# Selective scan of a graph network: steps alternate between the channel halves, decay factors in SBUF

## The reference, cut to what matters

```
dt  = softplus(dbc[:, :16] @ dt_proj_w.T + dt_proj_b)    # n x 256
Bm  = dbc[:, 16:32]; Cm = dbc[:, 32:]                    # n x 16 each
A   = -exp(A_log)                                        # 256 x 16
dA  = exp(dt[:, :, None] * A)                            # decay factors
dBx = (dt * xc)[:, :, None] * Bm[:, None, :]
def step(h, t):                                          # h: 256 x 16
    dA_t, dBx_t, C_t = t
    h = dA_t * h + dBx_t
    return (h, h @ C_t)
_, y = lax.scan(step, zeros, (dA, dBx, Cm))
y = (y + xc * D_param) * silu(z)
return y @ out_proj_w.T
```

## Time and profile before

| | us |
|---|---|
| median of 3 runs (7062.06 to 7075.2) | 7067.35 |
| the profiled execution's own time | 7078.49 |
| its span, from the first to the last instruction | 7076.8 |
| phase `mamb`: first load issued to the last projection | 2459.2 to 2877 |
| its loop: first scan to the end of the last product with C | 2469.76 to 2851.96 |

### The profile page before, as it was taken

The page is one execution under the profiler, slowest core; times in us unless marked ns, Lnnn a source line. Parts: engine busy times, 40 slices in busy tenths (PEclk is TensorE's granted clock), DMA queues, the critical chain, the costliest instruction groups (busy, mean ns, idle before and its releaser), DMA issues. The chain is left out here.

```text
span 7076.8 us, 83913 instructions
## 1 busy us (share of the span) xinstructions
PE 4376.6 (62%) x18956; PEld 2316.1 (33%) x18957; DVE 3988.4 (56%) x6332; ACT 1872.1 (26%) x2833; POOL 2303.0 (33%) x2173
## 2 busy tenths in 40 slices
PE   4888477233998266589656677456676444450387
PEld 2454366111443123465222333223333122220123
DVE  7987277598997699455222333122333122227998
ACT  1476111012886322244101111001111000110254
POOL 0000000410000066200466665666665666660000
PEclk8999687666999588799777888777887666665798
DMA  0471565434665377315555666555666444443444
GB/s 30 151 237 56 193 250 200 150 120 123 180 180 148 114 278 269 125 52 213 168 169 169 192 203 191 157 170 179 192 204 188 138 132 138 134 136 121 138 134 120
DMA packets 466391, 1139.22 MB, mean 161 GB/s; under 512 B 63000, under 2 KB 254255, under 8 KB 454409
## 3 DMA queue, kind: packets, MB, share of 16 engines
q1 hardware_dynamic: 294485, 543.98, 23.8%
q0 software_dynamic: 134816, 447.33, 21.3%
q10 hardware_dynamic: 36996, 146.80, 5.7%
HBM read 882.81 MB, written 258.28 MB: 161 GB/s over the span
## 5 line engine op out<-in xcount | busy, mean ns | idle before, releaser
L2693 POOL DMA_INDIRECT rel1s_rows<-rel_table,rel1s_at x640 | 625.7, 978 | 371.1 <-issue 289.0
L2693 POOL DMA_INDIRECT rel2s_rows<-rel_table,rel2s_at x640 | 616.0, 963 | 379.5 <-issue 222.1
L2693 POOL DMA_INDIRECT rel0s_rows<-rel_table,rel0s_at x640 | 625.7, 978 | 344.0 <-issue 284.6
L2895 PE MATMUL rel2s_acc<-rel2s_rows,rel2s_hot 128*128 x732 | 404.8, 563 | 483.2 <-issue 302.2
L2156 POOL TENSOR_TENSOR mamb_st<-mam_u,mamb_bc 128x1600 f32<-128x1600 f32 x64 | 236.7, 3699 | 1073.4 <-DMA mamb_bc<-dbc 1073.4
L1676 PE MATMUL gatx_acc<-gatx_w,gatx_feat 128*65 128x400 f32 x1600 | 541.3, 501 | 24.9 <-DVE gatx_w L1568 24.9
L2895 PE MATMUL rel0s_acc<-rel0s_rows,rel0s_hot 128*128 x732 | 317.8, 454 | 261.5 <-issue 183.1
L2895 PE MATMUL rel1s_acc<-rel1s_rows,rel1s_hot 128*128 x732 | 317.3, 452 | 238.9 <-issue 167.6
L1568 DVE SCALAR_TENSOR_TENSOR gatx_w<-gatx_w,gatx_adj 128x1600 f32<-128x1600 f32 x200 | 363.2, 1817 | 0.5 <-ACT gatx_w L1624 0.5
L1676 PE MATMUL latx_acc<-latx_w,latx_feat 128*65 128x400 f32 x800 | 291.0, 507 | 101.5 <-DVE latx_w L1568 101.5
L1415 DVE CUSTOM_DVE_ANT_0 gatm_junk<-gatm_srow,gatm_gone 128x3125 bf16<-128x3125 f32 x100 | 335.7, 3411 | 27.7 <-DMA gatm_srow<-gat_scores 23.4
(11 more groups left out here) (615 smaller groups left out, 9544.9 us busy)
## 6 DMA issues: line engine op xcount, KB each, us to landing
mamb_bc<-dbc SPq DMA_DIRECT2D x128, 800.0 KB, 5.6
agg_strip<-strips SPq DMA_DIRECT2D x100, 800.0 KB, 5.9
gatx_adj<-adj SPq DMA_DIRECT2D x200, 400.0 KB, 3.0
adj<-adj_counts SPq DMA_DIRECT2D x25, 1600.0 KB, 7.1
latx_adj<-adj SPq DMA_DIRECT2D x100, 400.0 KB, 3.1
rel_table<-rel0p_prod POOLq DMA_DIRECT2D x25, 1536.0 KB, 6.2
rel_table<-rel0s_prod ACTq DMA_DIRECT2D x25, 1536.0 KB
rel_table<-rel1s_prod ACTq DMA_DIRECT2D x25, 1536.0 KB
```

Source lines behind the costliest of these rows:

```text
L2693: pool.indirect_dma_start(rows[k][:, u, :], None, table, bass.IndirectOffsetOnAxis(ap=at[:, n:n + 1], axis=0)).then_inc(s_in[u], 16)
L2895: one = nc.tensor.matmul(acc[a][:, :], hots[k], most_two[k], start=fresh and k == 0, stop=False)
```

## The change

The 64 steps are ordered by node half, then state, then channel half: two steps in a row share their rows of B and C, which are loaded once for both (64 loads instead of 128; SP waits for the second of the two steps that used a buffer). Since two channel halves are now under way at a time there are two accumulators, which fill PSUM (4 banks each). The decay factors move from PSUM to SBUF, into two buffers of 128 x 1600, so that ACT waits for the scan two steps back. The last node half of both channel halves is now multiplied by silu(z) on DVE (8 instructions instead of 4), POOL has two output products in place of three, and the projection writes to the first accumulator.

```diff
@@ -2114,13 +2114,14 @@
-            acc = ph.ps("acc", [P, 4 * BANK])
-            dA = ph.ps("dA", [P, 4 * BANK])
+            dA = [ph.sb(f"dA{k}", [P, HALF]) for k in range(2)]
+            acc = [ph.ps(f"acc{ct}", [P, 4 * BANK]) for ct in range(2)]
...
-            todo = [(ct, half, n) for ct in range(2) for half in range(2) for n in range(S)]
+            todo = [(half, n, ct) for half in range(2) for n in range(S) for ct in range(2)]
+            rows = [(half, n, m) for half in range(2) for n in range(S) for m in range(2)]
@@ -2129,14 +2130,12 @@
-                for q, (ct, half, n) in enumerate(todo):
-                    for m in range(2):
-                        r = 2 * q + m
-                        if r >= RB:
-                            sp.wait_ge(s_hc if m else s_x, (r - RB) // 2 + 1)
-                        at = R + m * S + n
-                        sp.dma_start(bc[r % RB][:, :],
-                                     row(dbc_dram[at:at + 1, when(half)].rearrange("o n -> (o n)"))).then_inc(s_bc[r % RB], 16)
+                for r, (half, n, m) in enumerate(rows):
+                    if r >= RB:
+                        sp.wait_ge(s_hc if m else s_x, (r - RB) // 2 * 2 + 2)
+                    at = R + m * S + n
+                    sp.dma_start(bc[r % RB][:, :],
+                                 row(dbc_dram[at:at + 1, when(half)].rearrange("o n -> (o n)"))).then_inc(s_bc[r % RB], 16)
...
@@ -2146,84 +2145,82 @@
-                for q, (ct, half, n) in enumerate(todo):
-                    r = 2 * q
-                    if ct and not half and n == 0:
+                for q, (half, n, ct) in enumerate(todo):
+                    r = q // 2 * 2
+                    if q == 1:
                         pool.wait_ge(s_later, 2)
                     pool.wait_ge(s_bc[r % RB], 16 * (r // RB + 1))
                     if q >= RS:
                         pool.wait_ge(s_y, q - RS + 1)
                     nc.gpsimd.tensor_tensor(st[q % RS][:, :], u[:, ct, when(half)], bc[r % RB][:, :], ALU.mult).then_inc(s_x, 1)
-                    if q > S and n == 2:
-                        i = q // S - 1
-                        pool.wait_ge(s_copied, i + 1)
-                        at = when(i % 2)
-                        nc.gpsimd.tensor_tensor(yT[:, i // 2, at], yT[:, i // 2, at], dt[:, i // 2, at], ALU.mult).then_inc(s_yT, 1)
+                    if half and n == 2:
+                        pool.wait_ge(s_copied, ct + 1)
+                        nc.gpsimd.tensor_tensor(yT[:, ct, when(0)], yT[:, ct, when(0)], dt[:, ct, when(0)], ALU.mult).then_inc(s_yT, 1)
...
-                for q, (ct, half, n) in enumerate(todo):
-                    if ct and not half and n == 0:
+                for q, (half, n, ct) in enumerate(todo):
+                    if q == 1:
                         act.wait_ge(s_later, 2)
-                    if q:
-                        act.wait_ge(s_h, q)
-                    nc.scalar.activation(dA[:, 0:HALF], dt[:, ct, when(half)], ACT.Exp, scale=A[:, ct, n:n + 1]).then_inc(s_dA, 1)
-                    if q and n == 0:
-                        i = q // S - 1
-                        act.wait_ge(s_y, q)
+                    if q > 1:
+                        act.wait_ge(s_h, q - 1)
+                    nc.scalar.activation(dA[q % 2][:, :], dt[:, ct, when(half)], ACT.Exp, scale=A[:, ct, n:n + 1]).then_inc(s_dA, 1)
+                    if half and n == 0:
+                        act.wait_ge(s_y, 2 * S - 1 + ct)
                         for a, b in spans:
-                            last = nc.scalar.copy(dt[:, i // 2, (i % 2) * HALF + a:(i % 2) * HALF + b], acc[:, a:b])
+                            last = nc.scalar.copy(dt[:, ct, a:b], acc[ct][:, a:b])
                         last.then_inc(s_copied, 1)
...
-                                   dA[:, (q % 4) * BANK:(q % 4) * BANK + len(pr) * D]).then_inc(s_e, 1)
+                                   acc[0][:, (q % 4) * BANK:(q % 4) * BANK + len(pr) * D]).then_inc(s_e, 1)
...
-                for q, (ct, half, n) in enumerate(todo):
-                    r, tile = 2 * q + 1, st[q % RS]
+                for q, (half, n, ct) in enumerate(todo):
+                    r, tile = q // 2 * 2 + 1, st[q % RS]
                     dve.wait_ge(s_x, q + 1)
                     dve.wait_ge(s_dA, q + 1)
                     if half:
-                        dve.wait_ge(s_kept, ct * S + n + 1)
-                    nc.vector.tensor_tensor_scan(tile[:, :], dA[:, 0:HALF], tile[:, :], carry[:, ct, n:n + 1] if half else 0.0,
+                        dve.wait_ge(s_kept, 2 * n + ct + 1)
+                    nc.vector.tensor_tensor_scan(tile[:, :], dA[q % 2][:, :], tile[:, :], carry[:, ct, n:n + 1] if half else 0.0,
                                                  ALU.mult, ALU.add).then_inc(s_h, 1)
...
                         nc.vector.tensor_copy(carry[:, ct, n:n + 1], tile[:, HALF - 1:HALF]).then_inc(s_kept, 1)
-                        dve.wait_ge(s_kept, ct * S + n + 1)
+                        dve.wait_ge(s_kept, 2 * n + ct + 1)
                     dve.wait_ge(s_bc[r % RB], 16 * (r // RB + 1))
                     nc.vector.tensor_tensor(tile[:, :], tile[:, :], bc[r % RB][:, :], ALU.mult).then_inc(s_hc, 1)
-                dve.wait_ge(s_y, len(todo))
-                for a, b in spans:
-                    nc.vector.tensor_tensor(yT[:, 1, HALF + a:HALF + b], acc[:, a:b], yT[:, 1, HALF + a:HALF + b], ALU.mult).then_inc(s_yT, 1)
+                for ct in range(2):
+                    dve.wait_ge(s_y, len(todo) - 1 + ct)
+                    for a, b in spans:
+                        nc.vector.tensor_tensor(yT[:, ct, HALF + a:HALF + b], acc[ct][:, a:b], yT[:, ct, HALF + a:HALF + b],
+                                                ALU.mult).then_inc(s_yT, 1)
...
-                for q, (ct, half, n) in enumerate(todo):
+                for q, (half, n, ct) in enumerate(todo):
                     if n == 0:
-                        if q:
-                            pe.wait_ge(s_copied, q // S)
+                        if half:
+                            pe.wait_ge(s_copied, ct + 1)
                         for a, b in spans:
-                            nc.tensor.matmul(acc[:, a:b], diag[:, ct, :], xsT[:, ct, half * HALF + a:half * HALF + b], start=True, stop=False)
+                            nc.tensor.matmul(acc[ct][:, a:b], diag[:, ct, :], xsT[:, ct, half * HALF + a:half * HALF + b], start=True, stop=False)
                     pe.wait_ge(s_hc, q + 1)
                     for a, b in spans:
-                        last = nc.tensor.matmul(acc[:, a:b], g.ident[:, :], st[q % RS][:, a:b], start=False, stop=n == S - 1)
+                        last = nc.tensor.matmul(acc[ct][:, a:b], g.ident[:, :], st[q % RS][:, a:b], start=False, stop=n == S - 1)
                     last.then_inc(s_y, 1)
-                pe.wait_ge(s_h, len(todo))
-                pe.wait_ge(s_yT, 3)
+                pe.wait_ge(s_yT, 2 + len(spans))
...
-                        pe.wait_ge(s_yT, 3 + len(spans))
+                        pe.wait_ge(s_yT, 2 + 2 * len(spans))
...
-                            last = nc.tensor.matmul(dA[:, (q % 4) * BANK + n * D:(q % 4) * BANK + (n + 1) * D],
+                            last = nc.tensor.matmul(acc[0][:, (q % 4) * BANK + n * D:(q % 4) * BANK + (n + 1) * D],
```

## The result

| us | before | after |
|---|---|---|
| median (4 runs each) | 7064.86 | 7241.53 |
| runs | 7062.06 to 7075.2 | 7229.24 to 7243.47 |
| the profiled execution's span | 7076.8 | 7238.6 |
| loop, first scan to the end of the last product with C | 382.2 | 552.9 |
| its mean step | 5.97 | 8.64 |

The change makes the kernel slower: ratio 1.0244, 95% interval 1.0226 to 1.0261, 177 us between the medians. The loop alone grew by 170.7 us. (The two profiled spans differ by 162 us. The 9 us missing lie outside the loop: the stretch behind the last copy of this layer, where both kernels have the same code, took 4199.7 us before and 4189.6 after. Repeated executions of one kernel lie 13 and 14 us apart.)

A forecast was written before the change was run, and what follows sets the result against it. DVE was taken to bound the loop; 345 us own work plus 222 of POOL products less handovers gave 549 to 563, middle 556, +174; with +1 at the end, 7067 + 175 = 7242 us, range 7204 to 7264.

The forecast's parts named there:

- The scan joins what POOL excludes: Loop: with dA in SBUF the scan reads two SBUF tensors and must exclude POOL's product; +174 us.
- the handovers: Loop: start time hidden when DVE and POOL take turns; 18 us in all before the product with C, 4 after.
- The two places: Loop: POOL's product lies between scan and product with C (549 us) or after that product (563 us); PE decides.
- The forecast's signs: Loop: either products with C about 5.0 us with scans at 3.5, or scans about 6.8 with products at 1.8.
- Halved loads gain 0: Loop: 128 loads become 64, already hidden since DVE waits for none; 0 us on the path.
- Two accumulators, eight output products, the projection: Loop and end: accumulator sums and copies hidden, 0; output products and projection order 0; PE's clock at the end +1 us.
- PE's clock: Loop: PE's granted clock, 0.86 before the change, was expected at or under 0.86.
- B: Loop: scan not held, POOL's product falls on each product with C; 528 us, +146, 7213 us; chance 0.06.
- C: Loop: scan free, POOL asks in product with C, works under next scan; 36 us less, 7031 us; chance 0.05.
- D: Loop: B and C alternate, within 0.2% of before; chance 0.02, shared with a no-effect rival.
- The median: Whole kernel: median forecast 7067 + 175 = 7242 us, 2.5% slower.

The follow-up runs named there:

- the gate: Changed kernel plus a wait before POOL's product q for the product with C of step q-2: +164 us (one run), loop 546.3 us.
- the two gated kernels: POOL wait for product with C on kernel before with six buffers (0.9953, loop 358.1 us); on changed kernel, dA in PSUM, one accumulator (0.9963, 359.1 us).
- the kernels in which it could play: Changed kernel with dA in PSUM and one accumulator: 1.0075, loop 429.1 us; kernel before with six buffers for B and C: 1.0073, loop 442.0 us.

## Why the prediction was right

- *The scan joins what POOL excludes*, the main step, +174 us from 5.45 and 5.32 us of own work, 65 products of 3.41 us and the handovers: the loop grew by 170.7. Shown by moving dA alone (554.7 us) and by taking POOL's reading away (351.5).
- *The two places*, 549 us between scan and product and 563 after it: the first is now a measured kernel, 546.3 us with the gate. The second was not isolated. The middle was taken, 556; measured 552.9. What the forecast did not see is the form: not one handover a step but two POOL products in a row every second step, with nearly each pair holding one scan and one product, so that a step of 11.8 us follows one of 5.4. The forecast's signs (either the scan at 6.8 us or the product at 5.0) were each right for a part of the instructions of the changed kernel and not for all. The sum hardly changes by it, since each product is paid once: 65 were counted in the forecast, and 31 + 34 = 65 instructions were held.
- *Halved loads gain 0*: POOL's waits for them are gone and the two gated kernels differ by 1 us of loop.
- *Two accumulators, eight output products, the projection*: from the end of the loop to ACT's last copy 25.1 us in both kernels (2851.96 to 2877.1, 3023.85 to 3048.96). Forecast 0 for the first and +1 for PE's clock; it was 0, the last sum ran in 3.01 us.
- *PE's clock* at or under 0.86: 0.72.
- *Rivals B, C and D* were mis-sized, which cost nothing as their condition did not hold. B priced 62 held products, 528 us of loop; the kernels in which it could play had 429 and 442. A held step took 8.6 us there, where B had 8.34. D had the mixture of B and C within 0.2% of before; with the alternating order it was 0.75% slower.
- *The median*: 7242 forecast, 7241.5 measured. The closeness is luck in part: the profiled loop says +171, the medians +177. For the profiled execution, on which the sum was made, 7253 us were forecast and 7240.2 measured: the one before lay 11 us above its median, the one after 1 us below, and 10 of the 13 us lie behind this layer, in code that the change does not touch. And 556 us was the middle of two places that the forecast could not choose between.

## What to carry to other kernels

Before an operand moves from PSUM to SBUF, count what the instruction then reads: here every DVE scan or product with two tensors from SBUF and every POOL product, which reads SBUF too, ran one after the other, and both look busy while they wait. A long instruction that leaves POOL free is a place to put POOL's work, and it is worth a semaphore to put it there on purpose; here one wait and two buffers gave 0.5%, where freeing POOL of its late loads without that wait cost 0.7%. Where there is no such place, DVE, which makes the product in half of POOL's time, did better without help: a loop of 468.5 us against 552.9.

## What the runs showed of the hardware

A POOL fill of the same tile (1.43 us) and the two kinds of DVE instruction (3.48 and 1.82 us) run beside each other, though the fill writes 128x1600. A scan of 1600 elements takes 3.48 us with its decay factors in SBUF as in PSUM, as long as POOL makes no product beside it. Where both engines had work waiting, they took turns: in the changed kernel POOL's product ran between L2196 of 2615.31 and the scan of 2617.05, the next one between that scan and L2196 of 2624.38. A held instruction loses nothing at the handover: after the other's end it needs 1.68 instead of 1.82 us, 3.41 instead of 3.56. That its start has already been made by then is a reading of these numbers, and not shown.
